# A four-layer graph network on one core: turning aggregated rows and h by crossbar DMA instead of TensorE

## What is computed

```
layer 0: x += gated block of attention(h), state-space and feed-forward branches
layer 1: a = adj == 1;            x += ((a @ h) / a.sum(1)) @ W.T + b
layer 2: g = h @ W;  e = leaky(g @ a[:256] + (g @ a[256:]).T)
         x += elu(softmax(where(adj > 0, e, -1e12)) @ g)
layer 3: Q, K, V = h @ Wq, h @ Wk, h @ Wv;   x += softmax(Q @ K.T + mask(adj, diagonal)) @ V
```

## Time and profile before

| | us |
|---|---|
| median of three runs | 2314.56 |
| span of the profiled execution | 2312.6 |
| PE busy | 2213.7 (96%) |
| DVE busy | 1804.2 (78%) |
| ACT busy | 1380.9 (60%) |
| layer 1, loop over groups 1 to 7 | about 885 to 1171, 35.8 a group |
| layer 1, parts of the last group | 1171 to 1196 |
| layer 2, loop over groups 1 to 7 | about 1251 to 1599, 49.6 a group |
| layer 2, parts of the last group, then attention | 1599 to 2312 |

### The profile page before, as it was taken

The page is one execution under the profiler, slowest core; times in us unless marked ns, Lnnn a source line. Parts: engine busy times, 40 slices in busy tenths (PEclk is TensorE's granted clock), DMA queues, the critical chain, the costliest instruction groups (busy, mean ns, idle before and its releaser), DMA issues. The chain is left out here.

```text
span 2312.6 us, 45554 instructions
## 1 busy us (share of the span) xinstructions
PE 2213.7 (96%) x17148; PEld 1692.6 (73%) x17148; DVE 1804.2 (78%) x2833; ACT 1380.9 (60%) x2104; POOL 114.7 (5%) x124
## 2 busy tenths in 40 slices
PE   6899999999999998999978999999999999999999
PEld 4677767778776776888867888887466666666667
DVE  6977788797878856222249999997898898898897
ACT  6655565655656466666667555555465565665556
POOL 2000010010101001000000000000000000000000
PEclk9999999999999999999989999999999999999999
DMA  7542241414231012222211222222111111111010
GB/s 181 119 61 42 60 79 37 83 46 83 47 69 51 28 47 90 91 87 94 91 50 58 71 69 72 78 77 86 55 37 51 35 44 53 35 46 51 24 33 28
DMA packets 63414, 146.85 MB, mean 64 GB/s; under 512 B 10087, under 2 KB 15354, under 8 KB 62237
## 3 DMA queue, kind: packets, MB, share of 16 engines
q1 hardware_dynamic: 57037, 111.09, 15.3%
q0 software_dynamic: 5664, 33.16, 8.7%
q10 hardware_dynamic: 560, 0.52, 0.1%
HBM read 170.43 MB, written 41.43 MB: 92 GB/s over the span
## 5 line engine op out<-in xcount | busy, mean ns | idle before, releaser
L196 PE MATMUL bank<-s_row,kT_hi 128*128 128x512 f16 x1024 | 304.6, 379 | 5.7 <-ACT arena L2064 3.1
L2181 PE MATMUL bank<-VB,arena 128*128 128x257 f16 x1024 | 281.7, 275 | 15.4 <-ACT arena L2064 9.0
L1580 PE MATMUL bank<-VA,ph 128*128 128x257 f16 x1024 | 281.1, 274 | 6.9 <-DVE pl L1184 4.4
L1582 PE MATMUL bank<-VA,pl 128*128 128x257 f16 x1024 | 280.8, 274 | 0.0
L1581 PE MATMUL bank<-VA,ph 128*128 128x257 f16 x1024 | 280.8, 274 | 0.0
L2184 PE MATMUL bank<-VB,arena 128*128 128x257 f16 x1024 | 280.7, 274 | 0.0
L2182 PE MATMUL bank<-VB,arena 128*128 128x257 f16 x1024 | 280.4, 274 | 0.0
L2921 PE MATMUL bank<-VA,w_dense 128*128 128x257 f16 x1008 | 276.2, 274 | 3.0 <-ACT w_dense L2733 2.4
L2923 PE MATMUL bank<-VA,arena 128*128 128x257 f16 x1008 | 275.8, 274 | 0.0
L2922 PE MATMUL bank<-VA,w_dense 128*128 128x257 f16 x1008 | 275.8, 274 | 0.0
L2037 ACT CAST arena<-arena 128x512 f16<-128x512 f32 x256 | 158.2, 618 | 151.8 <-DVE arena L2092 141.3
(11 more groups left out here) (353 smaller groups left out, 4918.3 us busy)
## 6 DMA issues: line engine op xcount, KB each, us to landing
quad_ring<-mask_d SPq DMA_DIRECT2D x185, 256.0 KB, 2.7
mask<-mask_d SPq DMA_DIRECT2D x71, 256.0 KB, 2.8
mask_d<-in_adj POOLq DMA_DIRECT2D x8, 2048.0 KB, 23.5
xg<-in_x SPq DMA_DIRECT2D x8, 512.0 KB, 12.9
x<-xg SPq DMA_DIRECT2D x8, 512.0 KB, 3.9
xg<-x SPq DMA_DIRECT2D x8, 512.0 KB, 4.3
x<-xo POOLq DMA_DIRECT2D x8, 512.0 KB, 3.0
w_dense<-x SPq DMA_DIRECT2D x8, 512.0 KB, 4.2
```

The lines of the kernel that those rows point to most:

```text
L196: last = nc.tensor.matmul(out_ap, st, mv, start=(i == 0), stop=(i == len(todo) - 1))
L1580: nc.tensor.matmul(acc, ph[:, u % HR, c], v_row(V, 0, t), start=(t == 0), stop=False)
L1582: last = nc.tensor.matmul(acc, pl[:, u % HR, c], v_row(V, 0, t), start=False, stop=(t == T - 1))
L2181: nc.tensor.matmul(acc, p_hi, v_at(V, 0, t), start=first, stop=False)
```

## The change

Layers 1 and 2 no longer transpose `ag` and h on PE. ACT casts the rows as they lie in SBUF (one cast of 128x1024 instead of two of 128x512 from PSUM), DVE subtracts (one of 128x1024), and SP turns the two float16 halves with two crossbar transposes of 256 KB each (`dma_start(..., transpose=True)`), into a layout of 128x128 blocks. PE waits for these DMAs before `lin`, `wh` and the q and v products. In layer 2 the transposes write straight into kT, whose layout is now by tile, then half. The split of h moves from q = 5 to q = 4 in layer 1 and from q = 4 to q = 3 in layer 2. In program order on SP, the transposes stand behind the mask load of quad 5 (`ag`) and of quad 7 (h); as these loads run four quads ahead, that is when ACT or DVE is at quad 1 or 3. The first loads of the attention's masks and q on SP are moved ahead of the last group's parts of layer 2; the loads after them stay behind these parts.

```diff
@@ finish_layer1
-            pe_s.plan(("aT", K), ("lin", R), ("hT", K), ("wh", R))
+            pe_s.plan(("lin", R), ("wh", R))
@@ pe_beside
                     nc.tensor.wait_ge(s_later, 16 * 6)
+                    nc.tensor.wait_ge(act_s.sem, act_s.at(G - 1, "ag", R - 1))
@@ sync
+                if q == 5:
+                    sp.wait_ge(dve_s.sem, dve_s.at(g, "al"))
+                    sp.sem_inc(s_pass[3], 1)
+                    for p in range(2):
+                        sp.dma_start(aT[p][:, :, :], a_rows[p][:, :], transpose=True).then_inc(s_aT, 16)
+                if q == 7:
+                    sp.wait_ge(dve_s.sem, dve_s.at(g, "hl"))
+                    sp.sem_inc(s_pass[3], 1)
+                    for p in range(2):
+                        sp.dma_start(hT[p][:, :, :], h_rows[p][:, :], transpose=True).then_inc(s_hT, 16)
@@ act_part
                 if q == 1:
-                    for k in range(K):
-                        act.wait_ge(pe_s.sem, pe_s.at(g, "aT", k))
-                        hi(aT[0][:, k, :], bank[4 + k][:, :], "aT", k)
+                    act.wait_ge(act_s.sem, act_s.at(g, "ag", R - 1))
+                    act.wait_ge(pe_s.sem, pe_s.before(g, "lin", R - 1))
+                    hi(a_rows[0][:, :], ag[:, :], "ah", 0)
                 if q == 4:
                     normal(act, g, h, xo, nb, rsx)
-                if q == 5:
-                    for k in range(K):
-                        act.wait_ge(pe_s.sem, pe_s.at(g, "hT", k))
-                        hi(hT[0][:, k, :], bank[4 + k][:, :], "hT", k)
+                    act.wait_ge(act_s.sem, act_s.at(g, "h", R - 1))
+                    act.wait_ge(pe_s.sem, pe_s.before(g, "wh", R - 1))
+                    hi(h_rows[0][:, :], h[:, :], "hh", 0)
@@ dve_part
                 if q == 1:
+                    dve.wait_ge(act_s.sem, act_s.at(g, "ah"))
+                    lo(a_rows[1][:, :], ag[:, :], a_rows[0][:, :], "al", 0)
+                if q == 4:
+                    dve.wait_ge(act_s.sem, act_s.at(g, "hh"))
+                    lo(h_rows[1][:, :], h[:, :], h_rows[0][:, :], "hl", 0)
@@ pe_part
-                if q == 0:
-                    pe.wait_ge(act_s.sem, act_s.before(g, "wh"))
-                    for k in range(K):
-                        transposes(pe, bank[4 + k], lambda r: ag[:, r * D + k * P:r * D + (k + 1) * P],
                 if q == 2:
-                    pe.wait_ge(dve_s.sem, dve_s.at(g, "aT", K - 1))
+                    pe.wait_ge(s_aT, g * 32 + 32)
+                    pe.wait_ge(act_s.sem, act_s.before(g, "wh"))
-                if q == 4:
-                    for k in range(K):
-                        transposes(pe, bank[4 + k], lambda r: h[:, r * D + k * P:r * D + (k + 1) * P],
                 if q == 6:
-                    pe.wait_ge(dve_s.sem, dve_s.at(g, "hT", K - 1))
+                    pe.wait_ge(s_hT, g * 32 + 32)
@@ finish_layer2
+                if q == 7:
+                    sp.wait_ge(dve_s.sem, dve_s.at(g, "hl"))
+                    for p in range(2):
+                        sp.dma_start(kT[p][:, ds(g * (R * K * P), R * K * P)].rearrange("p (a n) -> p a n", n=P),
+                                     h_rows[p], transpose=True).then_inc(s_kT, 16)
@@ act_part
-                if q == 4:
-                    act.wait_ge(pe_s.sem, pe_s.at(g, "hT", K - 1))
-                    hi(columns(kT[0], g), psum[:, 4:6, :], "hT", 0)
+                if q == 3:
+                    act.wait_ge(act_s.sem, act_s.at(g, "h", R - 1))
+                    act.wait_ge(pe_s.sem, pe_s.before(g, "qT", K - 1))
+                    hi(h_rows[0], h, "hh", 0)
@@ pe_part
-                if q == 2:
-                    pe.wait_ge(dve_s.sem, dve_s.before(g, "v"))
-                    for k in range(K):
-                        transposes(pe, bank[4 + k], lambda r: h[:, r * D + k * P:r * D + (k + 1) * P],
                 if q == 5:
-                    pe.wait_ge(dve_s.sem, dve_s.at(g, "hT"))
+                    pe.wait_ge(dve_s.sem, dve_s.before(g, "v"))
+                    pe.wait_ge(s_kT, g * 32 + 32)
@@ fused_attention, SP
+                def beside(q):
+                    if q < 0:
+                        load_q(0)
+                        for n in range(slots):
+                            load_quad(n)
+                def rest(sp):
+                    load_q(1)
+                    load_x(0)
+                    for n in range(slots, G * quads):
```

More of the change, by code:

```diff
@@ L207, in cols, with blocks @@
             return t[0][:, k, r * P:(r + 1) * P], t[1][:, k, r * P:(r + 1) * P]
+        def blocks(t, r, k):
+            return t[0][:, r * K + k, :], t[1][:, r * K + k, :]
         def transposes(pe, dst, src, ready=None):
@@ L2010, in _ @@
                         sp.sem_inc(s_mask[i], 16 * len(range(i, skip, MS)))
-                    groups(sp, quad, work["sync"], None, None, work.get("sync_beside"))
+                    groups(sp, quad, work["sync"], None, None, (then or work).get("sync_beside"))
                     if "sync" in then:
@@ L2357, in sums_free @@
             def sums_free(act, g):
-                act.wait_ge(pe_s.sem, pe_s.before(g, "aT", K - 1))
+                act.wait_ge(dve_s.sem, dve_s.before(g, "al"))
             def pool_part(pool, g):
@@ L2424, in pe_part @@
                         products(pe, bank[6 + r // 2][:, (r % 2) * D:(r % 2 + 1) * D],
[L2425 removed]
+                                 [(blocks(aT, r, k), w("W1", k)) for k in range(K)]
                                  ).then_inc(pe_s.sem, pe_s.one("lin", r))
[L2427 to L2431 removed]
                 if q == 6:
[L2433 removed]
+                    pe.wait_ge(s_hT, g * 32 + 32)
                     for r in range(R):
                         products(pe, bank[4 + r][:, 0:D + 2],
[L2436 removed]
+                                 [(blocks(hT, r, k), w("W2", k)) for k in range(K)]
                                  ).then_inc(pe_s.sem, pe_s.one("wh", r))
@@ L2451, in finish_layer2 @@
             h = w_gate[1][:, 0:2 * R * D].bitcast(F32)
+            h_rows = [w_gate[p][:, 2 * R * D:3 * R * D] for p in range(2)]
+            s_kT = sem("l2_kT_turned")
             qT = spare[:, 4 * R * D:6 * R * D].rearrange("p (a k n) -> p a k n", a=2, k=K)
@@ L2474, in sums_free, with block, group_of @@
                 act.wait_ge(dve_s.sem, dve_s.before(g, "x"))
-            def columns(t, g):
-                return t[:, :, ds(g * GW, GW)]
+            def block(p, t, k):
+                return kT[p][:, ds(t * (K * P) + k * P, P)]
+            def group_of(p, g, k):
+                return kT[p][:, ds(g * (R * K * P), R * K * P)].rearrange("p (r k n) -> p r k n", r=R, k=K)[:, :, k, :]
             def own_values(p, g):
@@ L2672, in load_x @@
                     sp.dma_start(xg, x3_d[g * P:(g + 1) * P, :]).then_inc(s_xg, 16)
[L2674 to L2688, removed]
-                    sp.dma_start(out[(G - 1) * P:G * P, r * D:(r + 1) * D], row(res, r)).then_inc(s_end, 16)
-                sp.wait_ge(s_out, 16 * (G - 1))
-                sp.wait_ge(s_end, 16 * R)
+                def beside(q):
[7 more added lines that the diff above has]
+                    for n in range(slots, G * quads):
+                        load_quad(n)
+                        g, q = divmod(n, quads)
+                        if q == 4 and 1 <= g < G - 1:
+                            load_q(g + 1)
+                        if q == 6 and 2 <= g:
+                            load_x(g - 1)
+                    load_x(G - 1)
+                    for r in range(R):
+                        sp.wait_ge(end_rows.sem, end_rows.upto(r))
+                        sp.dma_start(out[(G - 1) * P:G * P, r * D:(r + 1) * D], row(res, r)).then_inc(s_end, 16)
+                    sp.wait_ge(s_out, 16 * (G - 1))
+                    sp.wait_ge(s_end, 16 * R)
+                return beside, rest
             def pool_program(pool):
@@ L2978, in pe_steps @@
                 return beside, rest
+            sp_beside, sp_rest = sp_steps(nc.sync)
             act_beside, act_rest = act_steps(nc.scalar)
@@ L2988, in build @@
         stream.close()
-        kT = [sb(top, f"kT_{p}", [P, K, N], F16) for p in ("hi", "lo")]
+        kT = [sb(top, f"kT_{p}", [P, T * K * P], F16) for p in ("hi", "lo")]
         arena.append(sb(top, "arena", [P, ARENA], F32))
```

58 lines of the change are left out of this document (25 added, 33 removed).

## The result

The changed kernel takes **2330.52 us**, the median of four runs (2329.26 to 2331.76), against 2314.76 us for the kernel before in its four (the three listed ahead and one of 2319.63): a ratio of 1.0070, with a 95% interval of 1.0058 to 1.0082. It is 15.8 us slower. The profiled execution took 2329.26 us and its span is 2327.6, 15.0 above the span of before. Where those 15.0 us arise can be read from time stamps in both timelines.

What follows compares the result with a forecast made beforehand. PE was taken to bound layer 1 and DVE layer 2. Layer 1's loop (-3.3 + 10.9), last parts (+18.2) and clock (+6.2) sum to +32.0 us, added to the median: 2346.6 us, range 2320 to 2440.

Steps and rivals of the forecast that it cites:

- the uncovered turns of the last parts: Last group's parts of layers 1 and 2: nothing covers three pairs of turns, 3D - 1.3, +18.2 us.
- ACT's new wait: Layer 1's loop, before quad 5: PE waits 1.27 us a group for mask casts behind ACT's new cast of h.
- the slow clock: Last groups' parts: PE's clock halves after new idle; +2.2 us at `lin`, +4.0 at q and v products, +6.2 together.
- the stall in layer 1's loop: Layer 1's loop: PE waits 1.55 us a group for turns longer than their covers, +10.9 us over seven groups.
- D: Time for a pair of turns, from the end of DVE's subtraction until PE may start; taken as 6.5 us.
- mine: The prediction's own case: D from 4.5 to 9 us, chance 0.61.
- the rival with turns as quick as plain transfers: Turns: D = 4.3 and no loop stall, +14.5 us, 2329; D = 3 without clock drop, 2319; chance 0.17.
- The upper bound: Size of D: write side in 32-byte pieces, 16384 at 10 ns, 10.2 us, giving D = 12.
- The first term: Layer 1's loop: of 1.74 us of transposes removed a group, 0.47 is left after ACT's wait, -3.3 us in seven.
- the cover: Layer 1's loop: PE work between DVE's subtraction and PE's need of the turns, 5.1 us for `ag`, 6.35 for h.
- Layer 2's loop: Layer 2's loop: 0.87 us of PE work a group removed where DVE is the limit; zero, group still 49.6 us.
- Small edits: PE's new wait before folding transposes, strided reads of h, moved attention and x loads: costed at zero.

Runs made afterwards that it cites:

- experiment 7: Changed kernel with one 512 KB turn instead of two of 256 KB in layer 1: 2330.4 us, ratio 1.0070 to the kernel before.
- experiment 2: Changed kernel with layer 1's cast of h on DVE instead of ACT: 2321.25 us, ratio 1.0029 to the kernel before.
- Experiment 1: Changed kernel with every pair of turns in layer 1 issued twice, first into scratch: 2367.36 us, ratio 1.0235 to the kernel before.
- experiment 4: Changed kernel with the last groups of both layers transposed by PE as before, loops keeping their DMAs: 2313.55 us, ratio 1.0001 to the kernel before.
- experiment 5: Changed kernel with only layer 1's last group transposed by PE: 2320.05 us, ratio 1.0032 to the kernel before.
- experiment 6: Changed kernel with only layer 2's last group transposed by PE: 2322.64 us, ratio 1.0039 to the kernel before.
- experiment 3: Changed kernel with a separate SP wait for each half, so the high half turns while DVE subtracts: 2325.51 us, ratio 1.0046 to the kernel before.
- experiment 8: Changed kernel with h cast on DVE in layer 1, a wait for each half and both last groups on PE: 2306.2 us, ratio 0.9965 to the kernel before.
- experiment 9: Changed kernel with h cast on DVE, split waits, layer 1's last group and all layer 2 groups on PE: 2305.84 us, ratio 0.9957 to the kernel before.

## Why the prediction came out as it did

The direction held, and so did the uncovered turns of the last parts, ACT's new wait and the slow clock; the size was twice too large, because the stall in layer 1's loop did not come. The 2330.5 measured lies within the range, 16 us below the number given. By the size of D the case that came true is mine, but only just, and that is luck: its condition was 4.5 to 9 and D is 4.6, and a group of layer 1, forecast at 36.9 us, took 35.35, where below 35.3 was to count as wrong. In what happened it is rather the rival with turns as quick as plain transfers: no stall in the loop, D near 4.3, 2329 us.

**D, the term that was mis-sized.** The prediction took 6.5 us, from 26 ns a packet, 2048 pieces for a pair, and "about a microsecond for the second issue on SP and for the mask load". The count was right but for 64 (2112); a packet took 20.9 ns; and the microsecond does not exist, since the issue runs beside the transfer (experiment 7), and D is the same 4.6 in the loop, with a mask load just ahead, as in the last parts of layer 1, with none. With 20.9 ns and without it, the same working gives 1.85 + 2.76 = 4.6. The 256 bytes a piece, which the prediction had assumed, came out: SP's queue moved 27.80 - 20.45 = 7.35 MB more for 28 turns of 1024 pieces. The upper bound, 32-byte pieces and D = 12, was far off: nothing in the earlier trace rows tied those short packets to a turn.

Of the Trainium skill's two statements, "Advanced Engine Details and Errata" (X-Bar Transpose (TRN2)) says that a transposing DMA is as fast as a plain one: for the time to landing the trace agrees, 3.2 to 3.3 us against 3.1 for a mask load of the same 256 KB in the same stretch (2.7 in the kernel before). For the DMA engines it doesn't, 1.38 us a turn against 0.85 for a plain 256 KB. The 1309 ns for a 128x128 block from the Trainium skill's "VectorE: DVE Perf Modes" (The three transpose paths) don't carry over to many blocks in one DMA: here sixteen took 4.6 us.

**Layer 1's loop**, forecast -3.3 + 10.9, measured -3.2. The first term was right to a tenth: the wait before quad 5 was forecast as 1.27 us and is 1.12, and experiment 2 took it away by its cause. That the two agree so closely is luck: the wait is 0.15 shorter than forecast, and 0.17 us a group stand elsewhere, not followed. The second is zero, because the stall is a difference: D = 4.6 lies 0.65 us under the cover of 5.27, D = 6.5 lies over both. Experiment 1 shows that the covers were read rightly.

**The last parts**, forecast 3D - 1.3 = 18.2, measured 12.42; the same formula with D = 4.6 gives 12.5. Here D counts in full, and a wrong D is wrong three times. Experiments 4 to 6 confirm that these three places make the loss.

**The clock**, forecast +6.2, measured +6.9. That the sum is close is luck, the places are not the ones named. `lin` had been forecast at 2.2. It ran at 0.50 all through and took 2.5 us longer, but only 1.96 reached the path: before, DVE was busy with other work until 1180.33 and took `lin`'s results late. The q and v products had been forecast at 4.0 and took 1.68: the clock came back while the twelve q products ran (4.44 us instead of 2.76), which the prediction had allowed for and taken too little of. The other 3.3 us lie in two stretches that it didn't name, the first scores and those behind the row of maxima.

**Layer 2's loop**, forecast zero, measured zero in its steady groups (49.59 and 49.58 us) and -1.6 in its first and last, where the prediction took the steady group for all. As its text had it, a group that changes would have made me wrong, and no steady one did.

**Small edits**, forecast zero: +0.7 us before the loop of layer 1 and -0.35 behind it, and by the stamps behind the account's table nearly all of both is spread or `wh`'s clock, and not the edits.

**What stays open.** In the changed kernel the first scores start at half clock after 3.10 us of idle time; in the kernel before they start after 3.06 us and run at full clock. In all variants but the last a part of them runs at half clock (idle 3.2 to 3.5 us); the last, with 2.36 us, is as the one before. The length of the idle time fits this order, but experiment 1 shows both clocks after nearly the same idle time, so it can't be all. Likewise the scores behind the row of maxima were slow where PE had idled 4.7 us before the q products (experiments 1, 2, 5, 7) and not where that was 3.4 us or gone (experiments 3, 4, 6, 8, 9); the runs show the order, not the cause.

## What to carry to other kernels

Moving transposes to a DMA trades PE time for latency: it gains where other work lies between the last write and the first read for as long as a pair of turns takes, and loses all of it in every tail where nothing does. So treat the steady loop and its last iteration as two cases, and keep the old way in the tail: that alone took back 16 us here. And ask what queues behind a new cast: the same cast on the engine with room was worth another 8.2 us (seven groups at 1.17), more than the 3.2 that the loop had gained without it.

## What the runs showed of the hardware

- A crossbar transpose of 128x1024 float16, SBUF to SBUF, is 1024 packets and 32 more of 20.9 ns each, 1.38 us on all 16 DMA engines, and lands 3.2 to 3.3 us after its issue begins. SP needs 1.23 to 1.36 us to issue it, four times a plain load's 0.33; twice the size in one instruction needs 1.7 to 2.0 and lands after 4.3. The DMA engines begin 1.2 us after the issue does.
- The turns lengthen the loads beside them, 256 KB from 2.7 to 3.1 us and 512 KB from 4.3 to 5.0.
- DVE casts 128x1024 float32 to float16 in SBUF in 0.69 us, ACT in 1.04, while DVE's subtraction of the same shape takes 1.23.
- A slow stretch of PE can stand well behind the idle time that goes with it: in the kernels with 4.7 us idle before the q products, these and the v products ran at 0.76 of full speed (after), and twelve matmuls 34 us behind them at 0.61, with no idle time over 1.2 us in between.
